# Fewer semaphore waits in a fused normalise, quantise and convolve kernel, and one wait moved from VectorE to TensorE

## What is computed

```python
def _gn(v, G=32, eps=1e-05):              # normalise each image over 32 groups of channels
    g = v.reshape(B_, G, C_ // G, H_, W_)
    m = jnp.mean(g, axis=(2, 3, 4), keepdims=True)
    s = jnp.var(g, axis=(2, 3, 4), keepdims=True)
    return ((g - m) / jnp.sqrt(s + eps)).reshape(v.shape)

def _L0_conv_ref(x, weight, lW, uW, lA, uA, gamma, beta, running_mean, running_var):
    identity = x
    xg = x.reshape(B, 4, 128, H, W)[:, [1, 2, 3, 0]]
    xa = round(clip((xg - lA) / (uA - lA), 0, 1) * 15) / 15
    wq = (round(clip((weight - lW) / (uW - lW), 0, 1) * 15) / 15 - 0.5) * 2
    y = einsum('bgihw,goi->bgohw', xa, wq.reshape(4, 128, 128)).reshape(B, C, H, W)
    inv = gamma / jnp.sqrt(running_var + 1e-05)
    y = relu(y * inv + (beta - running_mean * inv))
    return y + identity

out = x + _L0_conv_ref(_gn(x), ...)
```

## Time and profile before

| | before |
|---|---|
| time, median of 3 runs | 259.68 us (259.65 to 260.01) |
| time of the profiled execution | 259.98 us |
| span of the profiled execution | 258.3 us |
| instructions | 4030 |
| HBM read, written | 51.65 MB, 51.38 MB |
| mean granted TensorE clock | 0.906 |

### The profile page before, as it was taken

How to read it: one execution, slowest core, us unless ns; L and a number is a source line. 1 busy time by engine, 2 the same in 40 slices (tenths; PEclk the granted TensorE clock), 3 DMA queues, 4 the chain that set the end, 5 groups by cost and what they waited for, 6 DMA issues and landing times.

```text
span 258.3 us, 4030 instructions
## 1 busy us (share of the span) xinstructions
PE 190.6 (74%) x999; PEld 109.4 (42%) x999; DVE 229.5 (89%) x363; ACT 215.4 (83%) x394; POOL 213.5 (83%) x340
## 2 busy tenths in 40 slices
PE   1142995987788898668598787979966878998930
PEld 0132654553444555344364444454633535464410
DVE  2898698799999989999979999998999998999950
ACT  4338898889999998999978999989899997989600
POOL 6126869998999999899999999999989999989500
PEclk9999997699979779999859997986999995999995
DMA  6999999999999999999999999999999999999994
GB/s 216 394 413 411 409 407 410 415 415 419 416 417 415 413 416 417 413 417 418 412 417 417 416 418 417 412 415 416 415 417 417 416 413 408 402 399 393 381 385 158
DMA packets 34520, 103.28 MB, mean 400 GB/s; under 512 B 1202, under 2 KB 1730, under 8 KB 34498
## 3 DMA queue, kind: packets, MB, share of 16 engines
q1 hardware_dynamic: 18624, 54.86, 53.5%
q10 hardware_dynamic: 15874, 48.18, 46.8%
HBM read 51.65 MB, written 51.38 MB: 399 GB/s over the span
## 4 chain that ended last, share of the span: by engine, by line
POOL 35%; DVE 21%; PE 20%; issue 17%; DMA 2%; DVEq 1%; SPq 0%; POOLq 0%; ACT 0%
POOL images L411 17%; PE prod L594 14%; DVE images L482 9%; DVE stats L456 7%; POOL levels L421 6%; PE var_ps L584 5%; POOL dev L372 3%; DVE codes L471 3%; DMA images<-in_x 2%; POOL norm L399 1%; POOL dev L375 1%; POOL newt L395 1%; POOL scaled L401 1%; POOL newt L396 1%; POOL newt L397 1%
## 5 line engine op out<-in xcount | busy, mean ns | idle before, releaser
L594 PE MATMUL prod<-codes,w_t 128*128 128x392 bf16 x768 | 155.6, 357 | 18.1 <-DVE images L482 11.9
L482 DVE SCALAR_TENSOR_TENSOR images<-prod,floor,images 128x784 f32<-128x784 f32 x128 | 127.9, 1020 | 11.0 <-PE prod L594 10.8
L411 POOL TENSOR_SCALAR images<-images,coef 128x784 f32<-128x784 f32 x120 | 128.6, 1083 | 0.0
L594 PEld LDWEIGHTS prod<-codes,w_t 128*128 128x128 bf16 x768 | 76.4, 107 | 88.8 <-issue 43.1
L267 ACT ACTIVATE levels<-images,coef 128x784 int16<-128x784 f32 x95 | 91.5, 1028 | 0.4 <-POOL coef L403 0.4
L456 DVE BATCH_NORM_STATS2 stats<-images 128x6 f32<-128x392 f32 x136 | 68.9, 551 | 5.2 <-DMA images<-in_x 5.2
L240 ACT ACTIVATE unused<-images,sums 128x784 bf16<-128x784 f32 x60 | 56.1, 938 | 0.1
L234 ACT ACTIVATE unused<-images 128x784 bf16<-128x784 f32 x60 | 50.7, 846 | 6.2 <-DMA images<-in_x 5.1
L471 DVE TENSOR_SCALAR codes<-levels 128x3136 bf16<-128x3136 int16 x32 | 34.2, 1070 | 1.0 <-POOL levels L421 1.0
L421 POOL TENSOR_SCALAR levels<-images,coef 128x784 int16<-128x784 f32 x33 | 32.9, 997 | 0.1
L584 PE MATMUL var_ps<-dev,avg 128*128 128x8 f32 x128 | 21.9, 299 | 14.5 <-POOL dev L379 14.5
(11 more groups left out here) (66 smaller groups left out, 80.1 us busy)
## 6 DMA issues: line engine op xcount, KB each, us to landing
images<-in_x SPq DMA_DIRECT2D x30, 1568.0 KB, 13.2
out<-images ACTq DMA_DIRECT2D x30, 1568.0 KB, 17.5
images<-in_x SPq DMA_DIRECT2D x8, 392.0 KB, 6.6
out<-images SPq DMA_DIRECT2D x1, 1568.0 KB, 8.6
out<-images SPq DMA_DIRECT2D x4, 392.0 KB, 6.5
w_raw<-in_weight SPq DMA_DIRECT2D x1, 256.0 KB, 6.4
rows<-in_channel_params ACTq DMA_DIRECT2D x1, 8.0 KB, 2.4
limit_row<-in_limits ACTq DMA_DIRECT2D x1, 0.0 KB
```

What stands on the lines that cost most here:

```text
L411: nc.gpsimd.tensor_scalar(here, here, coef[:, u % 2, 0, 1, G * j + o:G * j + o + 1], coef[:, u % 2, 1, 1, G * j + o:G * j + o + 1], ALU.mu ...
L482: nc.vector.scalar_tensor_tensor(out=two, in0=prod[:, k % SETS, :, 0:HALF], scalar=floor[:, o:o + 1], in1=two, op0=ALU.max, op1=ALU.add).t ...
L594: done = nc.tensor.matmul(prod[:, k % SETS, h, 0:HALF], w_t[:, part, output_group(g)], codes[:, n % 2, g, h * HALF:(h + 1) * HALF], start= ...
```

## The change

Waits that an earlier wait on the same engine already implies are left out: ScalarE, GpSimd and VectorE wait for a load, for `squared`, `dev_done`, `var_done`, `coef_done` and `capped` once per image or once per pair of images, not once per group, and TensorE waits for `capped` in group 0 only. The wait for the affine pass leaves `finish` on VectorE and goes in front of the last of the six matmuls of the group on TensorE; `finish` then waits for `multiplied` alone, which is raised by that matmul. No arithmetic, no transfer and no order of work on an engine changes.

```diff
--- before.py
+++ after.py
@@ -225,10 +225,12 @@
 
             def take_sum(n, g):
                 u, j = n // 2, n % 2
-                wait_image(act, n, g)
-                if n:
+                first = g == stats_on_dve(u)
+                if first or n < SINGLE:
+                    wait_image(act, n, g)
+                if first and n:
                     act.wait_ge(squared, squares_before(n))
-                if u >= 2:
+                if first and j == 0 and u >= 2:
                     act.wait_ge(dev_done, u - 1)
                     act.wait_ge(var_done, u - 1)
                 nc.scalar.activation(unused[:, g % 2], images[:, n % RING, g], ACT.Identity, scale=1.0 / HW,
@@ -261,8 +263,9 @@
 
             def quantise(n, g):
                 u, j = n // 2, n % 2
-                act.wait_ge(coef_done, u + 1)
-                if n >= 2:
+                if g == 0 and j == 0:
+                    act.wait_ge(coef_done, u + 1)
+                if g == 0 and n >= 2:
                     act.wait_ge(capped, n - 1)
                 nc.scalar.activation(levels[:, n % 2, g], images[:, n % RING, g], ACT.Relu,
                                      bias=coef[:, u % 2, 1, 0, G * j + g:G * j + g + 1],
@@ -404,7 +407,6 @@
 
             def affine(n, g):
                 u, j, o = n // 2, n % 2, output_group(g)
-                pool.wait_ge(coef_done, u + 1)
                 if o < quant_on_act(n):
                     pool.wait_ge(q_act, (q_act_until(n - 1) if n else 0) + o + 1)
                 here = images[:, n % RING, o]
@@ -414,7 +416,8 @@
 
             def quantise(n):
                 u, j = n // 2, n % 2
-                pool.wait_ge(coef_done, u + 1)
+                if j == 0:
+                    pool.wait_ge(coef_done, u + 1)
                 if n >= 2:
                     pool.wait_ge(capped, n - 1)
                 for g in range(quant_on_act(n), G):
@@ -449,8 +452,9 @@
 
             def half_stats(n, g, h):
                 u, j = n // 2, n % 2
-                wait_image(dve, n, g)
-                if u >= 2:
+                if h == 0 and (g == 0 or n < SINGLE):
+                    wait_image(dve, n, g)
+                if (j, g, h) == (0, 0, 0) and u >= 2:
                     dve.wait_ge(dev_done, u - 1)
                 two = stats[:, u % 2, j, g, 2 * h:2 * h + 2].rearrange("p s k -> p (s k)")
                 nc.vector.bn_stats(two, images[:, n % RING, g, h * HALF:(h + 1) * HALF]).then_inc(bn_done, 1)
@@ -473,10 +477,6 @@
             def finish(n, g):
                 o = output_group(g)
                 k = G * n + g
-                if g < G - affine_on_act(n):
-                    dve.wait_ge(y_pool, (y_pool_until(n - 1) if n else 0) + g + 1)
-                else:
-                    dve.wait_ge(y_act, y_act_until(n - 1) + g - (G - affine_on_act(n)) + 1)
                 dve.wait_ge(multiplied, k + 1)
                 two = images[:, n % RING, o].rearrange("p (h f) -> p h f", h=2)
                 nc.vector.scalar_tensor_tensor(out=two, in0=prod[:, k % SETS, :, 0:HALF], scalar=floor[:, o:o + 1],
@@ -584,13 +584,23 @@
                     done = nc.tensor.matmul(var, avg[:], dev2[:, :, :, s], start=False, stop=(s == SUBSETS - 1))
                 done.then_inc(var_done, 1)
 
+
+            def wait_affine(n, g):
+                if g < G - affine_on_act(n):
+                    pe.wait_ge(y_pool, (y_pool_until(n - 1) if n else 0) + g + 1)
+                else:
+                    pe.wait_ge(y_act, y_act_until(n - 1) + g - (G - affine_on_act(n)) + 1)
+
             def multiply(n, g):
                 k = G * n + g
-                pe.wait_ge(capped, n + 1)
+                if g == 0:
+                    pe.wait_ge(capped, n + 1)
                 if k >= SETS:
                     pe.wait_ge(final, k - SETS + 1)
                 for part in range(PARTS):
                     for h in range(2):
+                        if (part, h) == (PARTS - 1, 1):
+                            wait_affine(n, g)
                         done = nc.tensor.matmul(prod[:, k % SETS, h, 0:HALF], w_t[:, part, output_group(g)],
                                                 codes[:, n % 2, g, h * HALF:(h + 1) * HALF],
                                                 start=(part == 0), stop=(part == PARTS - 1))
```

## The result

| | before | after |
|---|---|---|
| time, median of 11 runs each | 259.74 us | 258.78 us |
| its range | 259.51 to 261.27 | 258.05 to 259.06 |
| ratio, with its 95% interval | | 0.9946 [0.9931, 0.9962] |
| time of the profiled execution | 259.98 us | 258.41 us |
| VectorE's last instruction ends | 248.7 | 246.9 |

The change makes the kernel 0.54% faster: 1.0 us by the medians, 1.4 us by the ratio (interval 1.0 to 1.8). The forecast was 259.5. The time lies inside the stated range of 258.7 to 260.5, but outside the 259.16 to 260.20 to which I had given a chance of 0.70: what I had priced at 0.15 us is worth 1.0 to 1.4. Lines in after: L604 is the multiply (L594 before), L413 GpSimd's affine (L411), L475 cap (L471), L460 `bn_stats` (L456), L468 VectorE's sums (L464), L262 ACT's store (L260); finish stays L482.

What follows compares the result with a forecast made beforehand. The slowest DMA engine, with stores queued, was taken to set the end, compute having 3.8 us of slack. From the median of 259.68, terms of 0, 0 and 0.15 us gave 259.5, range 258.7 to 260.5.

Steps and rivals of the forecast that it cites:

- The bound: At the end of the span, the slowest DMA engine always has stores queued and sets the end; compute is ahead.
- The slack of compute: Before the slowest DMA engine begins image 30's store, compute was read as 3.8 us ahead.
- The advance of 1 to 2 us: VectorE's end was expected 1 to 2 us earlier through the waits left out, worth 0 at the end.
- (a): Covered waits left out on all compute engines, some 565 of 4030 instructions: compute gains 1 to 2 us, the end 0.
- (c): Fewer instructions fetched over DMA queues: 0.1 us if spread evenly, 1.7 if all on the slowest engine; taken as 0.15.
- (b): Affine wait moved from VectorE's finish to TensorE's last matmul: 17 late groups, 7.7 us in all, cost taken as 0.
- The slowest DMA engine is relieved, or compute does count: Rival at the end of the stores: fetches leave the slowest engine, or earlier compute closes DMA holes; 258.9, chance 0.17.
- signs for being wrong: ACT's queue empty at image 30's store, mid-span DMA share below 1, over ten low-clock stretches, last engine done a microsecond earlier.
- TensorE's clock: Rival: new holes inside matmul groups double the time at 1.2 GHz and delay compute; 263.8, chance 0.06.
- The order of transfers: Rival: stores issued at other moments change the load and store mix, 0.39 us an image; 260.1 to 260.5, chance 0.07.

Runs made afterwards that it cites:

- f2: The changed kernel with lighter arithmetic, plus 730 covered wait instructions on ScalarE alone; ratio to before 1.0042.
- h1: The kernel before with only VectorE's 226 wait instructions taken away (moved affine wait and half_stats); ratio to before 0.9980.
- j1: The changed kernel with eight more bn_stats on VectorE at image 8, 3.8 us of work; ratio to before 1.0048.
- h4: The changed kernel with 116 further instructions left out: more covered waits, and two sums per pair made one; ratio to before 0.9950.
- f1: The changed kernel with lighter arithmetic, plus 768 covered wait instructions on VectorE alone; ratio to before 1.0115.
- f3: The changed kernel with lighter arithmetic, plus 720 covered wait instructions on GpSimd alone; ratio to before 1.0021.
- h2: The kernel before with only the 341 wait instructions of ScalarE, GpSimd and TensorE taken away; ratio to before 0.9992.
- e1: The kernel before with only the affine wait moved from finish to the group's last matmul; ratio to before 0.9973.
- g1: The changed kernel with lighter arithmetic, multiplying one part of the weights instead of three, 1024 TensorE instructions fewer; ratio to before 0.9928.
- f4: The changed kernel with lighter arithmetic, plus 768 covered wait instructions on TensorE alone; ratio to before 0.9979.
- h3: The changed kernel with lighter arithmetic, plus three small memsets per finish on VectorE, 384 instructions without waits; ratio to before 1.0016.
- j3: The changed kernel at full compute, plus two covered wait instructions per finish on VectorE, 256 in all; ratio to before 0.9983.

## Why the prediction was wrong, and where it was right

**The bound: right.** The end is a DMA engine with work queued. The share stays at 1.02 to 1.04 until 240 us, the last microseconds show a few engines and then one, the slowest engine begins image 30 5 us after it was offered, and f2 and h1 end later than their partners by 2.0 and 0.8 us with VectorE's end unchanged.

**The slack of compute: right in sign, 3.8 us were too many** (j1: 1.2 by the ratios, 2.9 by the profiles; 2.6 in before by its own last store). It had no part in the error, since compute became earlier, not later. The advance of 1 to 2 us came (VectorE's end 248.7 to 246.9, 1.8 us). That it is worth 0 fits the 2.6 us of slack, and h4, whose VectorE ends 1.0 us after that of after with no loss; no run gives VectorE an earlier end and leaves the fetches alone.

**(a) Waits left out: right.** 3463 instructions against "some 3470"; neither L454 nor a wait of `finish` is left among VectorE's queued waits in the chain; work and busy times stay within 2%. What it gave compute is what I said; that these instructions are also bytes was term (c).

**(b) The moved wait: right in cost, wrong in count.** Four rows of after's timeline around image 13 (start us, us, engine, line, count):

```profile
118.98 4.70 POOL L413 TENSOR_SCALAR images<-images,coef 128x784 f32<-128x784 f32 x4
...
120.79 0.78 PEld L604 LDWEIGHTS prod<-codes,w_t 128*128 128x128 bf16 x6 [0.26 <-POOL images L413]
...
123.84 1.96 DVE L482 SCALAR_TENSOR_TENSOR images<-prod,floor,images 128x784 f32<-128x784 f32 x2
...
123.97 0.39 PE L575 MATMUL mean_ps<-sums,avg 128*128 128x4 f32 x2 [0.53 <-DVE sums L468]
```

The pattern is that of the earlier trace rows: the next weights are held up for 0.26 us behind the waiting matmul, and average_means still waits for VectorE's sums. The waits of the whole span (first two lines) and of 45 to 240 us (the rest), in after:

```profile
PEld prod L604 <- POOL images L413: 9.6, 33, 1.1
...
PE prod L604 <- POOL images L413: 1.2, 2, 0.7
```

```profile
DVE images L482 <- PE prod L604: 5.4, 10, 1.0
PE mean_ps L575 <- DVE sums L468: 5.3, 12, 0.5
PE prod L604 <- DVE images L482: 1.7, 4, 1.2
```

TensorE waits for the affine pass 33 times at its weights and twice at a matmul, some 10 us; I had counted 17 times and 7.7 us, on the timeline of before. VectorE does not pay: VectorE's wait for products falls from 7.9 us to 5.4, average_means waits as before. Idle time of TensorE changed its name.

**(c) Fewer fetches: the step that failed.** It says: 1.7 us if all lies on the slowest engine, 0.1 if it is spread, and takes 0.15 "near the even spread", although no row told which. The change is worth 1.0 to 1.4 us, near the other end. The 1.7 us were themselves taken from too much: they count both instruction queues, and q8 kept its 8 packets. What went is four packets of q14, and 4 x 0.30 us = 1.2 us is what a DMA engine would get back if all four lay on one. That this meets the measured value is in part luck: the light doses f1 to f3 put a packet at 0.28 to 0.70 us of the end and not at a sixteenth of 0.30, and by them the four (two of VectorE, one each of ScalarE and GpSimd, going by their counts of instructions) would be worth 2.1 us. The error was one of reasoning too: I had shown that the end is set by one lagging engine of 16, and then spread the load evenly over all of them, as if a load that falls on single engines could not be what makes one lag. The Trainium skill (Runtime: NRT & Kernel Launch, Instruction fetch mechanics), which calls the crossing of a fetch block mostly hidden, led the same way; by it the term is 0. It says so of the engine that fetches. What the runs show is the other side of it, a transfer on DMA engines that are full: 2.3 us at the end for 730 instructions on ScalarE. What is not closed: why a packet of VectorE costs more than its recorded time, why the parts h1 and h2 give less together than the whole, and how e1 gains 0.27% (down to 0.13% by its interval) with one fetch less.

**The rivals.** "The slowest DMA engine is relieved, or compute does count" (0.17, 258.9) came true in its first half, at 258.78; its second half has h4 and the slack against it, but no run of its own. Of the signs for being wrong two came: the last engine is done over a microsecond earlier (1.6 us), and the one of the clock. TensorE's clock (0.06): from 40 to 230 us fifteen stretches of 10 us lie below 1.00 and not ten, so the sign that I had named for it appeared, but they are shallower. They lack 2.21 and not 2.04 in all, which is 2.21 x 10 x 2 = 44 us at 1.2 GHz against 41, and nothing came of it at the end. The sign should have been the lacking sum, not the number of stretches. The page that the prediction names beside this rival (the Trainium skill, TensorE: Matmul & The Clock Gate, HAM oscillation) describes waits for DMA of some 3 to 5 us in each turn of a loop; the new waits here last 1.1 us at most, so this kernel is no test of it. The order of transfers (0.07): 409 and 417 GB/s in the mix as before, nothing moved.

## What to carry to other kernels

Where the DMA share is about 1.0 throughout, as here, instructions are also transfers on the same DMA engines, and a saving of instructions that hides beside compute can still come out at the end. Count the packets that go from q14 and price each at its time on one engine, not a sixteenth of it. Ask of a DMA-bound kernel which engine ends last and what makes it lag, since a mean over 16 hides both. To tell a compute effect from a DMA effect, compare kernels in which the last stores are issued at the same time, and look at the time from issue to landing; lighter arithmetic alone need not do it, as here it left VectorE's end where it was.

## What the runs showed of the hardware

- In this kernel, with light compute, an added instruction costs 5.4 ns of the launch on VectorE (f1), 3.1 on ScalarE (f2) and 2.4 on GpSimd (f3); on TensorE 0.7 (g1), or 0.8 with zero inside its uncertainty (f4). These are slopes over some 750 instructions; what is fetched comes in packets of 8 KB on q14, one for some 128 instructions.
- A fetch on q14 is recorded at 0.30 us of a DMA engine, but six of VectorE's cost the end 0.70 us each; a fetch on q8 is recorded at 0.88 us and costs some 0.2.
- Lag adds up: with 768 more instructions on VectorE the arrivals of one store spread over 7.0 us at image 20 in place of 2.5, and by 0.75 us for each further packet at image 22, whether waits (f1) or memsets (h3) are fetched. The last load is then complete 5.3 us later, and the DMA share falls to 0.92 in 220 to 240 us.
- A last store that has nothing queued ahead of it lands 6.0 to 6.2 us after its issue (j1, j3); in before it took 8.7.
